# Two re-orderings in a fused four-block transformer kernel: when sequences are weighed in the fourth attention layer, and when the statistics and roots of the norms are taken

## The reference

```
x = L0(x, cond, ctx, ...)   # self-attention (rotary, masked), cross-attention to 77 tokens, gelu MLP; adaptive layer norms
x = L1(x, cond, ctx, ...)   # prototype attention, router, three experts, gate
x = L2(x, ctx, cond, ...)   # cross-attention to 77 tokens, adaptive norm on both sides
x = L3(x, ctx, cond, ...)   # self-attention over 128 keys, cross-attention to 77 tokens, gelu FFN
```

## Time and profile before

| | us |
|---|---|
| three runs | 1119.22, 1119.86, 1120.95 |
| median | 1119.86 |
| profiled execution | 1120.89 |
| its span | 1119.1 |
| PE busy | 1041.9 (93%) |
| DVE busy | 787.6 (70%) |
| POOL busy | 683.6 (61%) |
| ACT busy | 583.6 (52%) |

### The profile page before, as it was taken

One profiled execution on the slowest core, in us unless ns is written; L12 is line 12 of the kernel. 1 busy time (PEld: TensorE's weight loads), 2 busy tenths in 40 slices (PEclk: granted clock), 3 DMA queues, 4 the chain that ended last, 5 costly groups with the idle time before them and its releaser, 6 DMA issues.

```text
span 1119.1 us, 28798 instructions
## 1 busy us (share of the span) xinstructions
PE 1041.9 (93%) x11743; PEld 652.9 (58%) x11743; DVE 787.6 (70%) x1949; ACT 583.6 (52%) x825; POOL 683.6 (61%) x784
## 2 busy tenths in 40 slices
PE   6899999999988999999999699999999999998998
PEld 4445555665654775666666445665555566654476
DVE  6778988778873535666677878888888766786321
ACT  1034444566666455444444256665555667765552
POOL 6568888688875331111205589987778666687430
PEclk8699999999999999999999889999999999999799
DMA  5210000000000112000000000000000000000001
GB/s 178 104 39 2 12 21 12 21 11 21 21 21 20 39 29 89 7 6 7 6 7 17 7 13 2 2 2 2 2 1 2 2 2 2 2 2 2 1 29 47
DMA packets 9282, 22.76 MB, mean 20 GB/s; under 512 B 1392, under 2 KB 1648, under 8 KB 8768
## 3 DMA queue, kind: packets, MB, share of 16 engines
q1 hardware_dynamic: 9152, 20.94, 5.6%
HBM read 18.77 MB, written 2.15 MB: 19 GB/s over the span
## 4 chain that ended last, share of the span: by engine, by line
PE 73%; DVE 12%; issue 5%; POOL 5%; ACT 4%; DMA 0%; DVEq 0%; POOLq 0%; ACTq 0%
PE weighed L657 11%; PE scores L630 9%; PE row_scores L599 7%; PE scores L842 6%; PE weighed L680 5%; DVE negmax L1153 5%; PE scores L556 4%; PE quads L538 3%; PE row_scores L842 3%; PE quads L563 3%; PE scores L642 2%; ACT p L1614 2%; PE quads L549 2%; PE scores L670 2%; PE weighed L853 2%
## 5 line engine op out<-in xcount | busy, mean ns | idle before, releaser
L1614 ACT ACTIVATE p<-scores 128x1024 f32<-128x1024 f32 (+1 forms) x256 | 247.7, 1018 | 208.9 <-PE scores L642 208.3
L1153 DVE TENSOR_REDUCE negmax<-row_scores 128x8 f32<-128x616 f32 (+1 forms) x312 | 299.0, 958 | 80.1 <-PE row_scores L599 62.2
L630 PE MATMUL scores<-qblk,work 32*77 32x512 f32 (+1 forms) x1280 | 206.8, 623 | 11.2 <-ACT p L1614 5.3
L657 PE MATMUL weighed<-p,v 77*32 77x128 f32 (+1 forms) x5120 | 175.5, 278 | 2.5 <-DVE nat L1178 2.5
L1786 POOL TENSOR_TENSOR kblk_r<-work,pack_const 128x308 fp32r<-128x308 f32 (+1 forms) x160 | 133.9, 838 | 69.5 <-PE row_scores L599 55.9
L1776 POOL TENSOR_TENSOR qblk<-work,pack_const 128x512 f32<-128x512 f32 x160 | 166.3, 1039 | 0.0
L599 PE MATMUL row_scores<-kblk_r,qr 32*128 32x308 f32 (+1 forms) x624 | 141.9, 445 | 24.7 <-DVE negmax L1153 23.8
L657 PEld LDWEIGHTS weighed<-p,v 77*32 77x32 f32 (+1 forms) x5120 | 131.8, 110 | 41.2 <-issue 37.2
L599 PEld LDWEIGHTS row_scores<-kblk_r,qr 32*128 32x128 f32 x624 | 62.1, 186 | 122.4 <-issue 93.3
L1178 DVE STREAM_TRANSPOSE nat<-weighed 128x256 f32<-128x256 f32 x160 | 71.0, 444 | 48.4 <-PE weighed L657 48.1
L1823 POOL TENSOR_TENSOR attn<-nat,rden 128x128 f32<-128x128 f32 x160 | 65.8, 411 | 51.9 <-DVE rden L1183 51.4
(11 more groups left out here) (299 smaller groups left out, 1887.5 us busy)
## 6 DMA issues: line engine op xcount, KB each, us to landing
shared<-gates_hbm SPq DMA_DIRECT2D x24, 256.0 KB, 3.3
shared<-in_ctx_tok SPq DMA_DIRECT2D x15, 154.0 KB
pack_w_l<-in_w_l SPq DMA_DIRECT2D x1, 2058.5 KB, 10.0
x<-in_x_tok SPq DMA_DIRECT2D x8, 256.0 KB, 5.8
out_x<-x SPq DMA_DIRECT2D x8, 256.0 KB, 2.0
layers_w<-in_w_l SPq DMA_DIRECT2D x1, 1289.0 KB, 7.9
ctxT<-in_ctxT SPq DMA_DIRECT2D x1, 1232.0 KB, 8.5
layers_w<-in_w_ada SPq DMA_DIRECT2D x1, 582.0 KB, 5.2
```

The costliest lines, as they stand in the source:

```text
L630: mm = e.matmul(scores[0:nk, g, :], k_of[q % 3][at, s * nk:(s + 1) * nk], qblk[n % 2][at, :], start=layer.mask != "qk", stop=False, skip_g ...
L657: mm = e.matmul(av_bank[TILE * j:TILE * j + TILE, i2 * S:(i2 + 1) * S], v[0:nk, at:at + TILE], p[n % 2][0:nk, g * NJ + j, :], start=i1 == ...
L1153: e.tensor_reduce(negmax[q % 2][:, 2 * h:2 * h + 2, s * NJ:(s + 1) * NJ], row_banks(n, h)[:, :, 0:NJ * nk].rearrange("p g (j k) -> p g j k ...
L1614: e.activation(p[n % 2][0:nk, 8 * h:8 * h + 8, :], scores[0:nk, 2 * h:2 * h + 2, :].rearrange("p g (j q) -> p (g j) q", j=NJ), ACT.Exp, bi ...
```

## The change

Five things are done.

1. `slots_of`: the fourth sequence of a family 1 norm is taken at slot - 2 (a second place), no longer at slot - 1.
2. PE, l3s only: `weigh(t - 1)` stands ahead of `quad_work` in the first, second and fourth place; in the third place it stays behind. l0 keeps its order, and so do the layers of 77 keys.
3. PE, l3s only: in the fourth place `turn_max` stands right behind `weigh` and ahead of the second half of the q projection; it was the last step of the place.
4. DVE, l3s only: `stats(t)` stands ahead of the hat, the residual and `turn_blocks(t - 1)`, as in l0; it was behind them.
5. ACT, all layers: the roots of a place stand ahead of its two exponentials; they were behind them and behind the copies.

```diff
@@ slots_of
     elif it.family:
-        at = [last - 1, last - 1, last, last + 1]
+        at = [last - 1, last - 1, last, last]
@@ tensor_program, attention
-                    if is_wide(t):
+                    if masked or is_wide(t) and cl == 2:
                         quad_work(t, qi, cl)
                         if t - 1 in jobs:
                             weigh(t - 1)
                     else:
                         ...
                         if cl == 3 and qi + 1 in quads:
                             turn_max(qi + 1)
                         quad_work(t, qi, cl)
-                    if is_wide(t) and cl == (2 if masked else 3) and qi + 1 in quads:
+                    if masked and cl == 2 and qi + 1 in quads:
                         turn_max(qi + 1)
@@ vector_program, attention
-                    if masked:
+                    if wide:
                         stats(t)
                     ...
-                    if not masked:
+                    if not wide:
                         stats(t)
@@ scalar_program, attention
                     roots = ROOT_AT.get((phase == 1, t), ())
+                    for it in roots:
+                        if t > 4 * hi:
+                            e.preload_act_table_set("natural_log_exp_and_others")
+                        root(it)
                     for h in range(2):
                         if t in jobs:
                             exponentiate(t, h)
                     ...
-                    for it in roots:
-                        if t > 4 * hi:
-                            e.preload_act_table_set("natural_log_exp_and_others")
-                        root(it)
```

## The result

The changed kernel took 1102.97 us (median of four executions, 1102.39 to 1104.04), the kernel before 1120.4 us beside it (four, 1119.22 to 1121.73): ratio 0.9848, 95% interval 0.9826 to 0.987. By these the gain is 15.8 us, and 1104.1 us lies inside the forecast range.

The account below looks back on a forecast made before the run. PE, busy 93% of the span, was taken as the bound. Order, roots and extra statistics summed to 7.4 us, plus 5.9 for the clock: 1119.86 - 13.3 = 1106.6 us, range 1103.5 to 1113.5.

Parts of the forecast that it names:

- All work of PE, DVE, ACT and POOL stays; only its order changes: Fourth layer: engines keep the same work; reordering alone gains 5.1 us, at most the 7.3 us PE waits.
- Weighing first costs nothing by itself: PE's sum stays: Fourth layer: weigh ahead of the quad's work leaves PE's sum unchanged, but hands a projection's bank over 1.0 us later.
- Second places: Fourth layer, quads 24 to 27: statistics ahead of nat start the maximum sooner, 4 x 0.34 = 1.36 us.
- First and fourth places: Fourth layer: earlier turn_max and weigh gain 2.0 us in first places; earlier statistics gain 1.10 and 0.6 in fourth places.
- l2 and l0c: One more DVE statistics pair in second places costs 0.8 us in l2, and 0.4 in l0c against 0.4 gained.
- Fifth layer and entry: Earlier roots gain 1.7 us in places 143, 147, 151, 0.9 at place 155, 0.95 entering l2; extra pairs cost 0.5.
- The clock at the end: Behind place 155: with the idle piece 0.8 us instead of 1.72, the clock stays at 1.00, gaining 5.9 us.
- A: Rival: the clock falls at the end all the same, or a little later; 1112.5 us, chance 0.17.
- B: Rival: the fourth layer's ping-pong between PE and DVE is not undone, only first places gain; 1109.7 us, chance 0.14.
- C: Rival: roots waiting for statistics stand in the path of ACT's exponentials; 1126.7 us, chance 0.04.
- D: Rival: the change does nothing measurable, since the early steps wait elsewhere; 1119.9 us, chance 0.03.
- A larger gain: Entry into l2: the clock also rises sooner, where about 2 us of half clock could go; the remaining chance, 0.02.

Follow-up runs that it names:

- e5: Changed kernel with turn_max in the fourth places of the fourth layer put back behind the quad's work: 1108.71 us.
- e1: Kernel before, with only PE's order in l3s changed (weigh ahead of the quad's work, turn_max earlier in fourth places): 1114.28 us, ratio 0.9971.
- e2: Kernel before, with only DVE's statistics in l3s put ahead of nat: 1115.32 us, ratio 0.9948.
- e3: Kernel before, with only the fourth sequence's statistics a place sooner and the roots ahead of the exponentials: 1111.31 us, ratio 0.9927.
- e9: Changed kernel, but four family 1 norms (slots 51, 55, 75, 79) keep the fourth sequence's statistics and root as before: 1103.81 us, ratio 0.9871.
- e6: Kernel before, with six filler multiplications on PE ahead of the 1.72 us wait in place 155: 1115.54 us, ratio 0.9962.
- e7: Changed kernel, with the one root of place 154 back behind the exponentials: 1108.83 us.
- e11: Changed kernel with four family 1 norms as before, plus three filler multiplications at the end of each of places 155 to 157: 1104.75 us, ratio 0.9863.
- e4: Kernel before, with the roots ahead of the exponentials but the fourth sequence's statistics left in their place: 1165.23 us, ratio 1.0413.
- e10: Changed kernel with four family 1 norms as before, plus three filler multiplications at the end of each of places 155 to 159: 1106.4 us, ratio 0.9861.

## Why the prediction was right, and where it failed

**The step "All work of PE, DVE, ACT and POOL stays; only its order changes" failed, and with it "Weighing first costs nothing by itself: PE's sum stays".** It is the largest part of the miss that the change itself made. The idle part of the step was right: PE's idle time in l3s fell by 4.66 us, and the forecast, without place 128, was 4.6. But PE's busy time fell as well, by 1.78 us, which the forecast put at nothing; its upper bound of 7.3 us was PE's idle time alone. With these 1.78 us added the time would be 1104.75 us, inside the range. The change of PE's order alone shows 1.65 of it. It is 0.14 us in each of eight fourth places, also in those that have no wait at all, and 0.06 to 0.08 in each first place from 100 to 124. Window of place 115 before and after:

```profile
885.65:890.02 4.37, 4.37 (x55) 2.28 (x53) 3.21 (x7) 2.54 (x4) 3.67 (x5) 1.00 0.00 0
```

```profile
877.25:881.47 4.22, 4.22 (x55) 2.30 (x53) 3.64 (x7) 2.63 (x3) 3.68 (x5) 1.00 0.00 0
```

The same 55 matmuls, PE busy throughout, 0.15 us less. e5 splits it: in the fourth place 0.05 is turn_max's place, the rest weigh's, and the first place's 0.07 is all turn_max's. Why the same matmuls take less in another order was not tested; by lines, L538 holds 0.4 us of the 1.78 (11.8 to 11.4), and the other lines' own times are the same within 0.1. The lines' times add up to 174.9 us before and 174.6 after, where PE is busy 137.16 and 135.38, so the rest is that the records of neighbouring matmuls overlap by some 1.5 us more.

**Second places, 1.36 us.** The size was right (4 x 0.32), the cause only half. e1 shows the same 0.32 with the statistics unmoved: with weigh ahead, nat comes sooner and so does all behind it. Either order is enough.

**First and fourth places.** First places gave 0.28 for the forecast 0.21 and all of it through turn_max (e5); place 128 gave 0.48 for 0.50. At places 120 and 124, taken as 0.4 and 0.05, it was 0.46 and 0.12. The statistics alone (e2) gave 0.62 in places 107 and 111 for 0.55, and 0.40 in 99 and 103 for 0.30.

**l2 and l0c, forecast +0.8 and 0.** The forecast cost is there: places 70, 74 and 78 grew by 0.25, 0.27 and 0.26. What the step put at nothing is what the earlier roots and statistics bring in fourth places: 67, 71 and 83 shrank by 0.29, 0.46 and 0.31, in e3 too. Place 83 doesn't gain by its own root, which stands ahead in e9 as well, where the place takes 4.13 us; its cause is a DVE instruction that gets shorter, shown in the last section. So l2 is 0.32 us shorter, 1.1 better than forecast. In l0c place 49 gained 0.56 for 0.4 and the stage 0.33.

**Fifth layer and entry.** Places 143, 147 and 151 went from 4.94 to 4.34 (0.60 for 0.57), and so did 142, by 0.12. The cost was larger than the forecast 0.5: 0.2 in each of 141 and 145, 0.09 in 146 and 0.40 in 150, 0.8 after the 0.12. Places 128 to 155 gave 1.53 with place 128, where the terms sum to 1.7. The entry gave 0.86 for 0.95, in a stage that also differs by itself: four executions without the early root have 313.0 to 314.5, all with it and the same statistics 311.9 to 313.3. The wait itself is gone: xh of the norm starts with no wait for a root. The clock there did not rise sooner; it stood at 0.50 for 17.1 us in the changed kernel's first profile and for 13.7 in its other two, as in the kernel before.

**The clock at the end, 5.9 us, measured 5.7.** Windows of the same 193 matmuls, from the exponentials of place 155 to those of 159: the kernel before, then e2 (nothing changed here), then the changed kernel.

```profile
1029.39:1050.19 20.80, 18.66 (x193) 9.53 (x197) 6.62 (x23) 8.23 (x10) 12.36 (x16) 0.59 0.00 1
```

```profile
1030.17:1045.26 15.09, 11.17 (x193) 6.22 (x197) 6.62 (x23) 8.22 (x10) 11.02 (x14) 1.00 0.01 2
```

```profile
1018.44:1032.49 14.05, 11.12 (x193) 6.22 (x197) 6.28 (x23) 8.22 (x10) 11.09 (x14) 1.00 0.01 2
```

20.80 - 15.09 = 5.7 is the clock, 15.09 - 14.05 = 1.04 the root (forecast 0.9). In the profile of before the granted clock is 0.50 from about 1032.6 to 1049.6 us; exact takes 2.00 us in it, beside 1.10 at 1.00. The 0.7 for the place behind is in the timeline too, where exact of place 159 takes 1.82 us beside the same 1.10:

```profile
1048.12 1.82 PE L630 MATMUL scores<-qblk,work 32*77 32x512 f32 x8
```

But the step took the loss of the kernel before for certain, and e2 shows an execution without it; that the two profiled executions gave nearly the forecast size is in part luck. Executions of the kernel before run from 1113.8 to 1125.5; the three known ahead of the forecast lay within 1.7 us and didn't show such a spread. What the traces show is that the same code at this place has a mean granted clock of 0.59 in one execution and 1.00 in another.

**The start, forecast 0, measured 1.47.** The profiled execution of the changed kernel reached place 0 after 60.45 us, the kernel before after 61.92. e3, with the same roots, has 61.82, e6, with the old ones, 60.49, and the changed kernel itself 63.70 in another execution. It is no effect of the change.

Sum by the profile, 1119.10 - 1101.39 = 17.71 us: start 1.47, l0c 0.33, entry 0.86, l2 0.32, l3s 6.43, places 128 to 155 1.53, behind it 6.75, the rest 0.02. Against the forecast 13.3 the 4.4 more are l3s 1.8, the start 1.5, l2 1.1, l0c 0.3, less small terms. Without the start and with the clock kept in both, the change is worth 17.71 - 1.47 - 5.7 = 10.5 us.

**The rivals.** A (the clock falls all the same) happened in none of the three profiled executions of the changed kernel, but its variants e7, e9 and e11 show that it can: e9, with the idle pieces of the changed kernel, and e11, with those of places 155 to 157 filled, lost it behind the last exponentials. B fell: L599 waits 2.2 us where 2.5 was written. C did not occur in the changed kernel, and e4 shows how near it was: it is what happens without point 1. D fell. A larger gain was given the 0.02 that is left, for a clock that rises sooner at the entry into l2; a larger gain came, but not from there.

## What to carry to other kernels

Where two engines alternate on one pair of banks, look for every instruction between the producer and the maximum on both; two re-orderings can mend the same wait, so price them together and test them apart. A root ahead of the exponentials needs statistics that are ready by then: with them a place sooner the change gained, without this it lost 46 us (e4). A stretch at half clock seen in one execution is a chance, not a term (0.59 here in one execution, 1.00 in another): look at more executions before it is counted, and put a filler in the kernel before to measure it by itself.

## What the runs showed of the hardware

**The clock.** In the profile of before the clock fell at 1032.6 us, near the end of an idle piece of PE of 1.72 us (1031.29 to 1033.01); in e1 it fell first near the end of one of 1.20 us, which the kernel before went through at full clock; in e9 and e11 it fell at the end of one of 1.23 us, while the changed kernel with e9's pieces kept it in three profiled executions. Of the four profiled executions with the piece of 1.7 us unfilled (before, e1, e2, e7) three lost the clock between the exponentials of place 155 and those of 159; of the eight in which the piece is shorter and the root and its statistics are early (three of the changed kernel, e3, e5, e9, e10, e11) none did, nor did e6 with its filler. e4, where the root waits for its statistics, is left out.

**Two small DVE instructions beside POOL.** Timeline of the kernel before, then of the changed one, in l2, where `spread_max` splits the maxima:

```profile
720.97 1.03 POOL L1776 TENSOR_TENSOR qblk<-work,pack_const 128x512 f32<-128x512 f32 x1
721.30 0.76 DVE L1161 CAST max_parts<-negmax 128x64 bf16<-128x64 f32 x1
721.97 0.69 POOL L1786 TENSOR_TENSOR kblk_r<-work,pack_const 128x308 fp32r<-128x308 f32 x1
722.09 0.66 DVE L1163 TENSOR_TENSOR max_parts<-negmax,max_parts 128x64 bf16<-128x64 f32 x1
```

```profile
718.58 0.71 POOL L1786 TENSOR_TENSOR kblk_r<-work,pack_const 128x308 fp32r<-128x308 f32 x1
718.60 0.74 DVE L1161 CAST max_parts<-negmax 128x64 bf16<-128x64 f32 x1
719.24 0.42 POOL L1823 TENSOR_TENSOR attn<-nat,rden 128x128 f32<-128x128 f32 x1
719.38 0.36 DVE L1163 TENSOR_TENSOR max_parts<-negmax,max_parts 128x64 bf16<-128x64 f32 x1
```

In l3s they take 0.15 and 0.32 us. The second ends 0.07 to 0.09 us behind the POOL instruction that was under way when it began (721.97 + 0.69 = 722.66, and 722.09 + 0.66 = 722.75), and how long it takes depends on that one: in the kernel before 0.23 us with none under way or with attn just begun (places 63 and 66), 0.32 to 0.36 beside attn, 0.65 beside kblk_r of 77 keys and 0.99 beside kblk_r of 128. The CAST ends with POOL's qblk or kblk_r in the same way, but takes 0.15 us beside attn, which runs on. Why they end with POOL's instruction, and why the CAST does so beside qblk and kblk_r and not beside attn, was not tested. What the rows show is that with another instruction of POOL under way, attn for kblk_r, DVE's second one takes 0.36 us in place of 0.66, and place 83 right behind these rows shows it. In the kernel before the maximum follows later, and the row scores wait for it; in the changed kernel they don't:

```profile
725.55 0.41 PE L599 MATMUL row_scores<-kblk_r,qr 32*128 32x308 f32 x2 [0.21 <-DVE negmax L1153]
```

```profile
722.56 0.40 PE L599 MATMUL row_scores<-kblk_r,qr 32*128 32x308 f32 x2
```

In all fourteen traces the two go together: where the second instruction takes 0.65 or 0.66 us in place 82, place 83 takes 4.08 to 4.14 us (before, e1, e2, e6, e9, e10, e11), and where it takes 0.36, 3.81 or 3.82 (the other seven). e9 differs from the changed kernel in l2 by the norms of slots 75 and 79 alone, so it is the move of their statistics and roots that made place 83 shorter.
